# A two-stage transformer kernel on one core: down products from high and low parts, and one input normalised a slot ahead

## The reference, cut to what matters

```python
x = x + 0.5 * moe(layernorm(x))         # "main" work
x = x + linear_attention(layernorm(x))  # "side", kind ATT
x = x + 0.5 * moe(layernorm(x))         # "main"
x = x + 0.5 * mlp(layernorm(x))         # "side", kind MLP
x = x + softmax_attention(layernorm(x)) # back end
x = x + 0.5 * mlp(layernorm(x))         # back end

def moe(x):   # 16 experts of 64, the best 2 by sigmoid score, and a shared one of 128
    g = silu(x @ We_gate); u = x @ We_up
    y = sum_e comb[:, e] * ((g * u)[e] @ We_down[e])
    return y + (silu(x @ Ws_gate) * (x @ Ws_up)) @ Ws_down
```

## Time and profile before

| | us |
|---|---|
| median of 3 runs | 1971.51 (1969.16 to 1973.76) |
| the profiled execution, own time | 1970.83 |
| span of its trace | 1969.0 |
| TensorE busy | 1879.2 (95%) |
| VectorE busy | 1533.5 (78%) |
| ScalarE busy | 1167.0 (59%) |
| GpSimd busy | 669.0 (34%) |
| mean granted TensorE clock | 0.989 of full |

### The profile page before, as it was taken

How to read it: one execution, slowest core, us unless ns; L and a number is a source line. 1 busy time by engine, 2 the same in 40 slices (tenths; PEclk the granted TensorE clock), 3 DMA queues, 4 the chain that set the end, 5 groups by cost and what they waited for, 6 DMA issues and landing times. The chain is left out here.

```text
span 1969.0 us, 34154 instructions
## 1 busy us (share of the span) xinstructions
PE 1879.2 (95%) x12340; PEld 1296.4 (66%) x12340; DVE 1533.5 (78%) x3824; ACT 1167.0 (59%) x2178; POOL 669.0 (34%) x768
## 2 busy tenths in 40 slices
PE   2999999999999999999999989999999999999996
PEld 2888888888888888888888844444444444444433
DVE  5776767676767776777677669999999999999991
ACT  2444444444444444444444328888888888888885
POOL 2333433343334333433343323333333333333311
PEclk9999999999999999999999969999999999999998
DMA  3000000000000000000010022222222222222210
GB/s 133 7 12 1 12 11 12 1 12 12 11 1 11 12 12 1 12 12 11 1 38 6 6 86 87 87 87 87 90 94 91 91 92 92 92 88 87 86 46 11
DMA packets 49991, 85.81 MB, mean 44 GB/s; under 512 B 6752, under 2 KB 11104, under 8 KB 49760
## 3 DMA queue, kind: packets, MB, share of 16 engines
q1 hardware_dynamic: 47920, 81.85, 13.0%
q10 hardware_dynamic: 1904, 1.78, 0.3%
HBM read 49.26 MB, written 34.87 MB: 43 GB/s over the span
## 5 line engine op out<-in xcount | busy, mean ns | idle before, releaser
L1528 DVE TENSOR_REDUCE b_nm<-b_MX 128x1 f32<-128x512 f32 x1024 | 648.6, 682 | 46.0 <-PE b_MX L1636 31.2
L1420 ACT ACTIVATE b_pr<-b_ST 128x512 f32<-128x512 f32 x1024 | 550.2, 603 | 101.0 <-PE b_ST L1624 96.7
L537 ACT ACTIVATE s<-G 128x512 f32<-128x512 f32 x306 | 182.6, 597 | 294.6 <-PE G L856 290.3
L691 DVE TENSOR_TENSOR su<-U,s 128x512 f32<-128x512 f32 x272 | 187.0, 687 | 208.7 <-PE U L856 106.4
L861 PE MATMUL Y<-w_wd,h 128*128 128x128 f32 x2448 | 328.2, 277 | 4.3 <-DVE h L700 4.3
L861 PEld LDWEIGHTS Y<-w_wd,h 128*128 128x128 f32 x2448 | 308.8, 192 | 26.7 <-DVE h L700 14.7
L1636 PE MATMUL b_MX<-b_kt,b_qt 32*128 32x512 f32 x768 | 240.6, 504 | 2.2 <-DVE b_nm L1528 1.8
L1624 PE MATMUL b_ST<-b_qt,b_kt 32*128 32x512 f32 x768 | 213.9, 494 | 6.1 <-ACT b_pr L1420 6.1
L1624 PEld LDWEIGHTS b_ST<-b_qt,b_kt 32*128 32x128 f32 x768 | 83.3, 181 | 203.8 <-ACT b_pr L1420 135.9
L700 DVE TENSOR_TENSOR h<-C,su 128x512 f32<-128x512 f32 x272 | 188.0, 691 | 9.3
L854 PE MATMUL G<-xh,w_wgh 128*128 128x512 f32 x306 | 145.5, 475 | 0.0
(11 more groups left out here) (295 smaller groups left out, 3629.7 us busy)
## 6 DMA issues: line engine op xcount, KB each, us to landing
b_kt<-staging SPq DMA_DIRECT2D x48, 256.0 KB, 2.7
b_qt<-staging SPq DMA_DIRECT2D x48, 256.0 KB, 3.0
staging<-e_khi SPq DMA_DIRECT2D x32, 256.0 KB, 2.9
staging<-e_qhi SPq DMA_DIRECT2D x32, 256.0 KB, 3.1
xin<-in_x SPq DMA_DIRECT2D x17, 256.0 KB, 2.8
mid<-xo SPq DMA_DIRECT2D x16, 256.0 KB, 2.0
staging<-e_klo SPq DMA_DIRECT2D x16, 256.0 KB, 3.0
staging<-e_qlo SPq DMA_DIRECT2D x16, 256.0 KB, 3.0
```

The lines of the kernel that those rows point to most:

```text
L537: nc.scalar.activation(sbuf_s[n % 2][:], G[n % 2][:], ACT.Silu).then_inc(act_done.sem, 1)
L691: nc.vector.tensor_tensor(out[:], U[:], sbuf_s[n % 2][:], ALU.mult).then_inc(up_used.sem, 1)
L1420: nc.scalar.activation(pr[k % 2][:, j], bank[:].rearrange("p a b -> p (a b)"), ACT.Exp, scale=SM_SCALE).then_inc(used["st"].sem, 1)
L1528: nc.vector.tensor_reduce(nm[g % 2][:, c:c + 1], bank[:].rearrange("p a b -> p (a b)"), AX.X, ALU.max).then_inc(used["mx"].sem, 1)
```

## The change

1. The down products of tiles 0 to 6 (NV = 7) are made transposed, into a bank V of their own: the weight (wdh, wdl, its high and low part, made in the setup) is stationary, and h moves, as hh and hl: V += wdh.hh + wdl.hh + wdh.hl, three f32r matmuls of 512 columns each. ScalarE makes hh (a copy to f32r: high), GpSimd makes hl = h - hh (low); both are rings of three tiles. Tiles 7 and 8 go to Y as before. At the end of a slot ScalarE copies V to vs (down_copy), and TensorE transposes vs into Y by four adding transposes (down_transposes), between the next slot's first gate product and the down product of tile 8.
2. moe_down lags by two tiles in place of one; at n = 8 tiles 6 and 7 are both done.
3. V takes the bank of G1: one bank G is left, and gate(n) waits for the silu of n - 1, not n - 2.
4. routed waits for hl_ready of the tile three back, not for down_done.
5. A MLP slot m now normalises two inputs: that of slot m + 1, and ahead of time that of slot m + 2 (its statistics at n = 5). The ATT slot between has neither statistics nor normalisation for its successor any more, and the routing of it stands earlier: transpose and low at n = 1, logits at 2, exp at 3, scores at 4, best 5, next 6, weights 7. In MLP slots the statistics stand at n = 1.
6. GpSimd's order is new (below), and xb is made by side_bias, later than side_start.
7. The side transposes stand behind moe_down at n = 2 in both kinds.

```diff
+NV = 7
+INPUT_STATS = 5
 PREPARE = {
-    MLP: {"statistics": 2, "transpose": 4, "low": 4, "logits": 5, "scores": 6, "best": 6, "next": 7, "weights": 8},
-    ATT: {"statistics": 1, "transpose": 3, "low": 3, "logits": 4, "scores": 5, "best": 6, "next": 7, "weights": 8},
+    MLP: {"statistics": 1, "transpose": 4, "low": 4, "logits": 5, "scores": 6, "best": 6, "next": 7, "weights": 8},
+    ATT: {"transpose": 1, "low": 1, "logits": 2, "scores": 4, "best": 5, "next": 6, "weights": 7},
 }
...
-        G = [ps(f"G{k}", [P, T, P]) for k in range(2)]
+        G = ps("G", [P, T, P])
+        V = ps("V", [P, T, P])
...
+            def low(m, n, i):
+                pool.wait_ge(hh_ready.sem, hh_ready.at(i, NV * m + n + 1))
+                nc.gpsimd.tensor_tensor(hl[n % 3][:], h[n % 3][:], hh[n % 3][:],
+                                        ALU.subtract).then_inc(hl_ready.sem, 1)
...
                     side_start(m, i, m)
-                    main_normalise(m + 1, i)
-                    if SIDE[m] == ATT:
+                    if SIDE[m] == MLP:
+                        lows(m, i, (0, 1))
+                        main_normalise(m + 1, i)
+                        lows(m, i, (2,))
+                        side_bias(m, i, m)
+                        lows(m, i, (3, 4))
+                        if has_input(m + 2, i):
+                            main_normalise(m + 2, i)
+                        lows(m, i, (5, 6))
+                    else:
                         a = nth(m)
+                        lows(m, i, (0, 1))
+                        side_bias(m, i, m)
+                        lows(m, i, (2, 3))
                         pool.wait_ge(ka_ready.sem, ka_ready.at(i, a + 1))
...
+                        lows(m, i, (4,))
                         pool.wait_ge(kvu_out.sem, kvu_out.at(i, T * (a + 1)))
...
+                        lows(m, i, (5,))
                         scale_offset(rstd2, off2, vpe2, mv2, mv2_ready, mv2_ready.at(i, a + 1), rstd2_ready)
+                        lows(m, i, (6,))
...
+            lows(0, turns, range(4))
             pool.wait_ge(early.mv_ready.sem, 1)
...
             nc.gpsimd.tensor_tensor(early.xn[:], early.xn[:], w["lnsb"][:], ALU.add).then_inc(early.xn_ready.sem, 1)
+            lows(0, turns, range(4, NV))
...
+            def high(m, n, i):
+                if n == 0:
+                    act.wait_ge(up_used.sem, up_used.at(i, NT * m + 1))
+                else:
+                    act.wait_ge(h_ready.sem, h_ready.at(i, TE * m + n))
+                nc.scalar.activation(hh[n % 3][:], h[n % 3][:], ACT.Copy).then_inc(hh_ready.sem, 1)
...
+                    if 1 <= n <= NV and n != 2:
+                        high(m, n - 1, i)
                     if n == 1 and side:
+                        if side == ATT:
+                            main_high(m + 1, i)
                         side_normalise(m, i, m)
                     if n == 2 and side:
                         side_high(i, m)
+                    if n == 2:
+                        high(m, n - 1, i)
...
+                down_copy(m, i)
...
                 if n >= 3:
-                    dve.wait_ge(down_done.sem, down_done.at(i, g0 + n - 2))
+                    dve.wait_ge(hl_ready.sem, hl_ready.at(i, NV * m + n - 2))
...
+                        if n == INPUT_STATS and side != ATT and has_input(m + 2, i):
+                            main_stats(m + 2, i)
...
             def moe_down(m, n, i):
-                if n == 0:
+                if n < NV:
+                    high, low = hh[n % 3], hl[n % 3]
+                    pe.wait_ge(hh_ready.sem, hh_ready.at(i, NV * m + n + 1))
+                    pe.matmul(flat(V), w["wdh"][:, n], flat(high), start=(n == 0), stop=False, skip_group_check=True)
+                    pe.wait_ge(hl_ready.sem, hl_ready.at(i, NV * m + n + 1))
+                    pe.matmul(flat(V), w["wdl"][:, n], flat(high), start=False, stop=False, skip_group_check=True)
+                    pe.matmul(flat(V), w["wdh"][:, n], flat(low), start=False, stop=True,
+                              skip_group_check=True).then_inc(down_done.sem, 1)
+                    return
+                if n == NV:
...
+            def down_transposes(m, i):
+                pe.wait_ge(vs_ready.sem, vs_ready.at(i, m + 1))
+                for t in range(T):
+                    pe.matmul(Y[:, t], vs[:, t], w["ident"][:], start=False, stop=True, is_transpose=True,
+                              skip_group_check=True)
...
-                if n >= 2:
-                    pe.wait_ge(act_done.sem, act_done.at(i, g0 + n - 1))
-                elif n == 0:
+                if n >= 1:
+                    pe.wait_ge(act_done.sem, act_done.at(i, g0 + n))
...
-                    if n >= 1:
-                        moe_down(m, n - 1, i)
+                    if n >= 2:
+                        moe_down(m, n - 2, i)
+                    if n == NT - 1:
+                        moe_down(m, NT - 2, i)
+                    if n == 2 and side:
+                        side_transposes(i, m)
...
                 if prepare:
                     gate(m + 1, 0, i)
+                down_transposes(m, i)
                 moe_down(m, NT - 1, i)
...
+            wait_loads(act, "down")
+            nc.scalar.activation(w["wdh"][:], w["wd"][:, 0:NV], ACT.Copy)
```

More of the change, by code:

```diff
@@ L227, in build_front @@
         h = [sb(f"h{k}", [P, T, P]) for k in range(3)]
+        hh = [sb(f"hh{k}", [P, T, P], F32R) for k in range(3)]
+        hl = [sb(f"hl{k}", [P, T, P], F32R) for k in range(3)]
+        vs = sb("vs", [P, T, P])
         kvu = sb("kvu", [P, T, 3 * D])
@@ L277, in build_front @@
         down_done = sig("down_done", NT * NM, NT)
+        hh_ready = sig("hh_ready", NV * NM, NV)
+        hl_ready = sig("hl_ready", NV * NM, NV)
+        vs_ready = sig("vs_ready", NM, 1)
         main_done = sig("main_done", NM, 2)
@@ L323, in build_front, with has_input @@
         block = ctx.enter_context(nc.Block())
+        def has_input(q, i):
+            return q < NM or i < turns - 1
         def source(q):
@@ L412, in main_normalise @@
             def main_normalise(q, i):
+                if zT_ready.at(i, q) > 0:
+                    pool.wait_ge(zT_ready.sem, zT_ready.at(i, q))
                 rsqrt(rstd[:, :, 0], vpe, mv, mv_ready, mv_ready.at(i, q + 1), rstd_ready)
@@ L419, in main_normalise, with lows, side_bias @@
                 nc.gpsimd.tensor_tensor(z[:], z[:], rstd[:].broadcast_to([P, T, D]), ALU.mult).then_inc(z_ready.sem, 1)
+            def low(m, n, i):
+                pool.wait_ge(hh_ready.sem, hh_ready.at(i, NV * m + n + 1))
+                nc.gpsimd.tensor_tensor(hl[n % 3][:], h[n % 3][:], hh[n % 3][:],
+                                        ALU.subtract).then_inc(hl_ready.sem, 1)
+            def lows(m, i, tiles):
+                for n in tiles:
+                    low(m, n, i)
             def side_start(m, i, k):
                 scale_offset(rstd_s, off_s, vpe_s, mv_s, smv_ready, smv_ready.at(i, k + 1), srstd_ready)
+            def side_bias(m, i, k):
                 pool.wait_ge(side_done.sem, side_done.at(i, k))
@@ L428, in _ @@
             main_normalise(-1, 0)
+            own.step(nc.gpsimd.tensor_tensor(w["wdl"][:], w["wd"][:, 0:NV], w["wdh"][:], ALU.subtract))
+            own.settle()
             main_normalise(0, 0)
+            lows(-1, 0, range(5))
+            main_normalise(1, 0)
+            lows(-1, 0, range(5, NV))
             own.step(nc.gpsimd.memset(early.va[:], 0.0))
@@ L562, in slot @@
                     if prepare:
-                        if n == steps["transpose"]:
+                        if n == steps["transpose"] and side != ATT:
                             main_high(m + 1, i)
@@ L602, in main_stats @@
             def main_stats(q, i):
+                if z_ready.at(i, q) > 0:
+                    dve.wait_ge(z_ready.sem, z_ready.at(i, q))
                 if q % 2 == 1:
-                    p = MAIN_BATCH[q]
-                    dve.wait_ge(x_loaded[p].sem, x_loaded[p].at(i, 32 if q == 3 else 16))
+                    p = MAIN_BATCH[q % NM]
+                    dve.wait_ge(x_loaded[p].sem, x_loaded[p].at(i + q // NM, 32 if q % NM == 3 else 16))
                 elif q == 0:
@@ L798, in slot @@
                     if prepare:
-                        if n == steps["statistics"]:
+                        if n == steps.get("statistics"):
                             main_stats(m + 1, i)
@@ L980, in gate @@
                         pe.wait_ge(act_done.sem, act_done.at(i, g0))
-                product(G[n % 2], w["wgh"][:, n], w["wgl"][:, n], xh[m % 2], xl[m % 2]).then_inc(gate_ready.sem, 1)
+                product(G, w["wgh"][:, n], w["wgl"][:, n], xh[m % 2], xl[m % 2]).then_inc(gate_ready.sem, 1)
             def slot(m, i, side, prepare):
@@ L1001, in slot @@
                         down(S[1], oT, w["wout"][:], True).then_inc(side_mm.sem, 1)
-                    if n == 2 and side == MLP:
```

(3 more changed lines are left out.)

14 lines of the change are left out of this document (7 added, 7 removed).

## The result

The changed kernel takes 2101.4 us (median of 4 runs, 2098.0 to 2105.0) where the kernel before takes 1971.7 on the same chip: ratio 1.0659, 95% interval 1.0636 to 1.0682. It is 130 us slower; 57 us were forecast, and the range ended at 2055. The profiled execution took 2098.0, its span is 2096.2, 127.2 us over that of before.

A forecast was written before the change was run, and what follows sets the result against it. The front was taken as bound by TensorE's list of work. 16 ATT slots at 3.2 us (51), closing slot +7 and opening slot -1 gave +57, so 2028 us, range 1945 to 2055.

The forecast's parts named there:

- the main mechanism: ATT slot: GpSimd's operations hold routing_best, mask_heads stands behind it, so the attention product waits 3.2 us.
- The query product's wait: ATT slot: Exp issued at n = 3 delays ScalarE's later work and the queries' bank; TensorE waits 1.1 us.
- Rival 1: Front end: TensorE stays the bound because the new queues keep ahead; faster, 1947 us; chance 0.25.
- rival 2: ATT slots: the attention wait is short, 0.7 to 1.5 us; 1988 us in all; chance 0.14.
- The saving of 0.92 us a slot: TensorE, every front slot: V products save 1.4 us, transposes into Y cost 0.44; 31 us in 34 slots.
- What follows it at half rate: ATT slots: the 3.2 us wait lowers TensorE's clock, costing 2 us each time, +32, 2060 us; chance 0.08.
- the late wait for h(8) is gone: End of ATT slot: the 0.22 us wait vanishes, as 1.1 us more work stands ahead of that product.
- The walk: Followed a slot through the four engine queues with profiled durations: ATT slot +3.2 us, MLP slot 0.
- my rule "with two SBUF inputs": VectorE operations with two SBUF inputs wait for the running GpSimd operation to end and enter at the boundary.
- The MLP slot: Sum 0: saving 0.92 and an old 0.3 wait, against new waits of 0.3, 0.5 (z) and 0.45 (low(2)).
- The opening slot: First front slot: saves 0.9 us, the weight parts lying in the setup; taken as -1 +- 1.
- The closing slot: Last front slot: GpSimd does lows 0 to 3 before early's 6.5 us chain, delaying the back end: +7 once.

The follow-up runs named there:

- Experiment 1: Changed kernel with routing_best of the ATT slots moved from n = 5 to n = 6, behind mask_heads: 2047.7 us, ratio 1.0377.
- experiment 5: Changed kernel without GpSimd's subtractions, the third V product taking the high part again (wrong result, same TensorE work): 2017.2 us, ratio 1.0225.
- experiment 10: Kernel before with only the input normalised a slot ahead and its routing moved (routing_best at tile 5), down products unchanged, no subtractions: 2013.2 us, ratio 1.0210.
- experiment 2: Changed kernel with 12 useless matmuls on TensorE while it waits ahead of the attention product: 2080.4 us, ratio 1.0550.
- experiment 3: Changed kernel with the ATT slot's routing from scores on a tile later (scores 5, best 6, next 7, weights 8), exp at 5: 2003.0 us, ratio 1.0151.
- Experiment 7: Changed kernel with the ATT routing a tile later and, in MLP slots, the next input's reciprocal root ahead of low(1): 1985.0 us, ratio 1.0062.
- experiment 12: Changed kernel, repeat run: ATT routing later, root ahead of low(1), opening slot's low(0), low(1) first, early chain in last MLP slot: 1965.2 us, ratio 0.9963.
- experiment 4: Changed kernel with low(0) and low(1) ahead of the opening slot's normalisation, and the closing slot's chain after low(1): 2089.4 us, ratio 1.0596.

## Why the prediction was right and wrong

**The direction and the main mechanism held, the time did not.** routing_best goes through only at the ends of GpSimd's operations, mask_heads stands behind it, and attention waits 3.2 us: forecast 3.2, measured 51.2 / 16. Experiment 1 shows the order, experiments 5 and 10 that GpSimd's operations of the ATT chain alone make 2.1 to 2.2 us of it. The rule that the prediction cites from the Trainium skill, "SBUF — State Buffer", section "Who interferes with whom", agrees with these rows (0.09 us from each end). The query product's wait was forecast at 1.1 and measured at 0.9, the spacing of V's matmuls at 0.23. Rival 1 fell by the wait itself, rival 2 too. (The saving of 0.92 us a slot should read 0.96 by its own terms, 7 x 0.20 less 0.44; that is 1 us in all.)

**The step that failed first is the clock.** The sum forecast a standstill of 3.2 us and priced it as 3.2 us. What follows it at half rate stood among the rivals, at 0.08, since the rows showed one such fall outside the front. It came in 15 of 16 ATT slots; its price was put at 2 us and is 1.4 net (experiment 2); against the slots of the same run in which the clock did not fall it is 1.0 in experiment 1 and 2.0 in experiment 5. A wait of that length and its clock belong in one term: 15 x 1.4 = 21 us of the 70 by which the span is beyond the forecast. By itself this would have given 2049, still inside the range; the three terms that follow took the time out of it. The Trainium skill, "TensorE: Matmul & The Clock Gate", section "Why this matters for your kernels", which I had set against one row, was right here, in 15 of 16 slots: 44 windows below 0.95 where the kernel before has none.

**That the late wait for h(8) is gone was wrong.** It was argued from TensorE's work alone. The walk stopped at attention, and did not follow routing_weights, which the change moves to tile 7. There the subtraction of hl(6) holds its first addition (by 0.8 us in the slot shown, by 0.3 to 0.9 in the others), and two of the operations behind it, the cast always among them, meet GpSimd's two og operations: h(8) is late by 1.0 to 1.7 us in each slot, 20.8 us in all, 17 more than before. It is gone both where routing_weights stands at tile 8 (0.4 us left, experiment 3) and where the subtractions are left out (experiment 5). The cast and the copy have one SBUF input, which my rule "with two SBUF inputs" left out; the same section of the Trainium skill that I cited, "SBUF — State Buffer", "Who interferes with whom", names copy and cast among those that can contend, and the rows agree at 1.30 and 1.33 us where both take 0.20 in experiment 5, ahead of og.

**The MLP slot**: forecast 0, measured +0.97. The places were right (z, 0.3 us forecast as 0.5; low(2), 0.35 as 0.45), the sum was not, since a wait costs more than its idle time: after the two waits of 0.35 us TensorE's next start is late by 0.5 and 0.6. Experiment 7 took out 1.2 us a pair with them. The saving of the products is there, but smaller than the count: in experiment 5, where no listed wait is left, the MLP slot is 0.6 us shorter than before, where 0.92 was counted and a wait of 0.2 less besides. For the pair 1.84 were forecast, and experiment 12 has 0.29. Listed waits hardly tell the two apart (0.9 us a pair there, 0.8 before), so the rest lies in what is not listed as idle, and its causes stay open.

**The opening slot** was taken as -1 and is +6.9 (6.5 from the first silu on). I had costed its TensorE work, not GpSimd's queue, in which the normalisation of the next input waits for statistics ahead of low(0): experiment 4 takes out 4.7. **The closing slot** was forecast at +7 and is +8.4; this was the one end where the queue was read.

In all: 57 forecast; 21 for the clock, 17 for h(8), 16 for the MLP slots, 8 for the opening slot and 1 for the closing one make 120 of 127. The last 7 stay open.

## What to carry to other kernels

Follow each moved step to its last instruction, not only to the first wait that it makes: here routing_weights cost 17 us two tiles after the place that was walked with care. When an engine at 98% of its time is made to stand still for some microseconds, price the wait and the half clock behind it together. And if a helper on a slow, in-order engine is put among others, place each piece against the time at which it is wanted; 2101 and 1965 us are the same arithmetic in another order.

## What was not expected of the hardware

A standstill of about 2 us does not always bring the low clock: after 2.11 us in experiment 1 the next window has 1.00, and the clock fell in 6 slots of 16; after 2.10 us in experiment 10 it is 0.50, and it fell in 15. After 3.2 us in the changed kernel it fell in 15 too. TensorE ran at full rate through the waits for h(8) of up to 1.8 us in experiment 2.

VectorE's operations with one SBUF input, of only 64 elements per partition, are held until GpSimd's operation over 128x512 ends: cast 1.30 us, copy 1.33, and an addition of a constant (L698) 1.29, where they take 0.2 alone; reductions stay at 0.22 and the reciprocal at 0.55 beside the same GpSimd work. Not every long GpSimd operation holds VectorE: beside the reciprocal root over 128x4, 1.04 us from 615.28 on, VectorE's operations with two SBUF inputs take 0.22 and 0.23 (615.59 and 615.73).
